# Weights in other areas, a ring of four weight slots, and the second product one block behind the first

## The reference

```python
x = x + L0_xcond(...)   # three rounds of slot attention
x = x + L0_ffn(...)     # 8 experts, top 2, all computed
x = x + L1_xcond(...)   # 16 heads of 64, over 512 + 77 keys
x = x + L1_ffn(...)     # 8 experts, each token to the one with the largest gate
x = x + L2_xcond(...)   # attention over itself, over the context, and a gated FFN
x = x + L2_ffn(...)     # 16 experts and a shared one
x = x + L3_xcond(...)   # 6 layers: attention, cross attention, FFN
x = x + L3_ffn(...)     # half of the tokens through an FFN
```

```python
logits = xf @ Wg + bg                      # xf: tokens, D = 128; Wg: 128 x 8
one_hot = jax.nn.one_hot(jnp.argmax(logits, axis=-1), e)
h = jax.nn.gelu(jnp.einsum('td,edh->eth', xf, W1), approximate=True)   # H = 512
y = jnp.einsum('eth,ehd->etd', h, W2)
out = jnp.einsum('etd,te->td', y, one_hot)
```

## Time and profile before

| what | value |
|---|---|
| median of 3 runs | 4170.21 us (4165.55 to 4171.18) |
| the profiled execution, its own time | 4145.95 us |
| its span from first to last instruction | 4144.1 us |
| mean granted TensorE clock | 0.949 |
| TensorE busy | 3599.2 us (87%) |
| VectorE busy | 2465.0 us (59%) |
| ScalarE busy | 2296.2 us (55%) |
| GpSimd busy | 1355.3 us (33%) |
| bytes moved by DMA | 146.41 MB, mean 35 GB/s |

### The profile page before, as it was taken

One profiled execution on the slowest core, in us unless ns is written; L12 is line 12 of the kernel. 1 busy time (PEld: TensorE's weight loads), 2 busy tenths in 40 slices (PEclk: granted clock), 3 DMA queues, 4 the chain that ended last, 5 costly groups with the idle time before them and its releaser, 6 DMA issues.

```text
span 4144.1 us, 56756 instructions
## 1 busy us (share of the span) xinstructions
PE 3599.2 (87%) x22327; PEld 1596.7 (39%) x22327; DVE 2465.0 (59%) x4758; ACT 2296.2 (55%) x3200; POOL 1355.3 (33%) x1355
## 2 busy tenths in 40 slices
PE   5699999899568988998895889898999998988886
PEld 4477433333443344334552233233333332333333
DVE  6732444544225345543658877777778677777754
ACT  4543554454124554545321766777767676776683
POOL 5500233333224511441003234344343442433411
PEclk8699999999799999999896999999999999999998
DMA  2000000000330010001111101111111110110100
GB/s 118 1 21 1 31 16 22 6 16 22 128 109 11 17 32 27 16 17 56 39 27 44 36 25 38 52 27 45 43 32 40 43 47 25 43 47 25 41 12 16
DMA packets 126956, 146.41 MB, mean 35 GB/s; under 512 B 36141, under 2 KB 107637, under 8 KB 124866
## 3 DMA queue, kind: packets, MB, share of 16 engines
q1 hardware_dynamic: 125664, 140.67, 11.5%
q0 software_dynamic: 1024, 2.10, 0.2%
HBM read 74.63 MB, written 6.43 MB: 20 GB/s over the span
## 4 chain that ended last, share of the span: by engine, by line
PE 59%; DVE 22%; ACT 8%; POOL 5%; DMA 3%; issue 3%; SPq 1%; POOLq 0%; DVEq 0%; ACTq 0%
PE ps L1903 6%; PE ps L1919 6%; PE ps L2114 6%; DVE c1sm L2862 4%; DVE c0sm L2862 4%; PE ps L2031 3%; PE ps L1823 3%; PE ps L1815 3%; PE ps L2100 3%; ACT wB L2358 2%; PE ps L2058 2%; PE ps L1951 2%; PE ps L1844 2%; PE ps L2158 2%; POOL c1m L3043 2%
## 5 line engine op out<-in xcount | busy, mean ns | idle before, releaser
L2358 ACT ACTIVATE wB<-ps 128x1024 f32<-128x1024 f32 (+1 forms) x762 | 762.1, 1022 | 270.0 <-PE ps L2100 263.8
L2862 DVE TENSOR_REDUCE c1sm<-ps 128x2 f32<-128x1024 f32 x384 | 456.6, 1220 | 128.1 <-PE ps L2058 125.3
L2862 DVE TENSOR_REDUCE c0sm<-ps 128x2 f32<-128x1024 f32 x384 | 453.2, 1219 | 97.2 <-PE ps L2058 95.3
L2656 DVE TENSOR_REDUCE c1sm<-ps 128x2 f32<-128x1024 f32 x128 | 151.7, 1220 | 194.0 <-PE ps L1868 192.8
L2656 DVE TENSOR_REDUCE c0sm<-ps 128x2 f32<-128x1024 f32 x128 | 152.5, 1221 | 172.3 <-PE ps L1868 171.3
L2358 ACT ACTIVATE c0m<-ps 128x1024 f32<-128x1024 f32 (+1 forms) x198 | 202.4, 1022 | 70.0 <-PE ps L2100 68.0
L2114 PE MATMUL ps<-wB,c1m 128*18 128x512 f32 (+1 forms) x1216 | 205.5, 611 | 1.1 <-DVE c1sm L2869 0.6
L1903 PE MATMUL ps<-c0ar 64*128 64x512 f32 (+1 forms) x640 | 178.1, 634 | 20.8 <-DVE c0sm L2656 9.1
L2100 PE MATMUL ps<-c0ar 64*128 64x512 bf16 (+1 forms) x864 | 167.0, 388 | 33.0 <-DVE c1sm L2862 14.4
L2100 PE MATMUL ps<-c1ar 64*128 64x512 bf16 (+1 forms) x864 | 165.3, 392 | 26.5 <-DVE c0sm L2862 9.2
L2992 POOL TENSOR_SCALAR c0sm<-c0sm 128x4 f32<-128x4 f32 x40 | 7.8, 194 | 547.9 <-DVE c0sm L2430 462.5
(11 more groups left out here) (918 smaller groups left out, 8268.1 us busy)
## 6 DMA issues: line engine op xcount, KB each, us to landing
c0ar<-c0m SPq DMA_DIRECT2D x216, 128.0 KB, 2.4
c1ar<-c0m SPq DMA_DIRECT2D x216, 128.0 KB, 2.4
c0m<-rscr SPq DMA_DIRECT2D x96, 128.0 KB, 2.9
c1m<-rscr SPq DMA_DIRECT2D x96, 128.0 KB
wA<-in_lay SPq DMA_DIRECT2D x6, 1346.0 KB, 5.6
c0ar<-in_x SPq DMA_DIRECT2D x15, 512.0 KB, 3.5
c1ar<-in_x SPq DMA_DIRECT2D x15, 512.0 KB
wA<-in_w SPq DMA_DIRECT2D x1, 4248.0 KB, 22.0
```

The source lines that it names most:

```text
L2358: e.activation(P.ap[0:n, :, :], u.ap[0:n, :].rearrange("p (a q) -> p a q", a=2), ACT.Exp, scale=S8).then_inc(*A(("P8", n0, s, k), free=[u]))
L2656: e.tensor_reduce(c.sm[:, 2 * (g % 2), 2 * j:2 * j + 2], u.ap.rearrange("p (h k) -> p h k", h=2)[:, :, 0:n], AX, ALU.max, negate=True).the ...
L2862: e.tensor_reduce(c.mneg[:, j, :, s // 4, s % 4], u.ap.rearrange("p (a k) -> p a k", a=2), AX, ALU.max, negate=True).then_inc(*V(free=[u]))
```

## The change

1. Stage 3 has a ring of four weight slots in place of three. The fourth takes the place of one of three token buffers and of free columns of the arena. The second product follows one block behind the first, not two.
2. `w4b` is split: the second attention's weights go to `wB`, the FFN's (`w4f`) to `wA` beside the first attention's (`w4a`). So `w4a` and `w4f` are loaded at the end of stage 1, `w4b` at the end of stage 2, `w5` goes to `wA`, the last FFN's `w7` to `wB`.
3. The layers of stage 6 use `wB` and `wA` in turn. Layer 0 is loaded at the end of stage 4 as before, layer 1 at the end of stage 5. The free columns that stage 6 shares out give seven buffers of 512 columns and not six.
4. A load of weights is now a step that the planner places by its clocks (`loads`), and a stream does not enter a stage before its load stands in the list.
5. The planner's numbers are new for all stages (`ORDER`; one of seven pairs of lines is shown).

Lines of the changed kernel from the planning part on have numbers up to 15 higher.

```diff
-    "3": dict(lag=0.0447, weight=0.2689, even=0, held=0.1381, table=0.6108, apart=9.6377, spread=0, seed=6349, bias=dict(TA=0.2, T=-0.615, S=1.124, VG=-1.263, TVb=-0.505, TAV=0.396, TV=1.124, V=0.115, A=0.392, G=-0.208), turns=((155, 662, 1.0), (397, 673, 0), )),
+    "3": dict(lag=0.0447, weight=0.2689, even=0.0203, held=0.1381, table=0.6108, apart=9.6377, spread=0, seed=6349, bias=dict(TA=0.2, T=-0.615, S=1.124, VG=-1.263, TVb=-0.505, TAV=0.396, TV=1.124, V=0.115, A=0.392, G=-0.208), turns=((47, 359, 0.3), (155, 662, 1.0), (397, 673, 0), )),
...
-        W4A, W4B, W5, W7 = view(wB, W4A_COLS), view(wA, W4B_COLS), view(wB, W5_COLS), view(wA, W7_COLS)
-        WL = [view(wA[:, k * LCOLS:(k + 1) * LCOLS], LAY_COLS) for k in range(2)]
+        W4A, W4B, W5, W7 = view(wA, W4A_COLS), view(wB, W4A_COLS), view(wA, W5_COLS), view(wB, W7_COLS)
+        W4F = view(wA[:, 4224:], W4F_COLS)
+        lay_at = [wB[:, 0:LCOLS], wA[:, 0:LCOLS]]
+        WL = [view(a, LAY_COLS) for a in lay_at]
         SEL = wA[:, 7200:8224]
...
-            r.B = Bufs([a[:, o:o + 512].rearrange("p (k d) -> p k d", k=4) for o in (1024, 1536, 2560)])
-            r.wring = [a[:, 5376 + 1024 * k:6400 + 1024 * k] for k in range(3)]
+            r.B = Bufs([a[:, o:o + 512].rearrange("p (k d) -> p k d", k=4) for o in (1024, 1536)])
+            r.wring = [a[:, o:o + 1024] for o in (2560, 5376, 6400, 7424)]
...
-        VC = [wA[0:NCTX, 2 * LCOLS + 1024 + 864 * k:2 * LCOLS + 1888 + 864 * k].rearrange("p (b q r) -> p b q r", b=NB, q=8)
+        VC = [wA[0:NCTX, LCOLS + 864 * k:LCOLS + 864 + 864 * k].rearrange("p (b q r) -> p b q r", b=NB, q=8)
...
-        spare = [[wA[:, 0:WA_COLS], 2 * LCOLS + 2752], [wB, 0], [areas[0][:, 0:5632], 0], [areas[1][:, 0:5632], 0],
+        spare = [[wA[:, 0:WA_COLS], LCOLS + 1728], [wB, LCOLS], [areas[0][:, 0:5632], 0], [areas[1][:, 0:5632], 0],
...
+        PACK = {"1": "w1", "2": "w2", "3": "w3", "4": "w4a", "5": "w5"}
+
+        def loads(pack, area, f):
+            yield from do("load", pack, area, f, chain=[("S", .4)], after=max(plan.clock[k] for k in "TAVG"))
+            issued.add(pack)
...
+                while PACK[name] not in issued:
+                    yield
                 if name not in begun:
                     begun[name] = c
                     if name != "1":
                         plan.stage(name)
-                    emit("gate", {"1": ("w_w1", "w1"), "2": ("w_w2", "w2"), "3": ("w_w3", "w3"), "4": ("w_w4a", "w4a"),
-                                  "5": ("w_w5", "w5")}[name])
+                    emit("gate", ("w_" + PACK[name], PACK[name]))
...
-                        emit("load", "w3", "wC", "1")
-                        emit("load", "w4b", "wA", "1")
+                        for pack, area in (("w3", "wC"), ("w4a", "wA"), ("w4f", "wF")):
+                            plan.spawn(loads(pack, area, "1"))
                     elif name == "2":
-                        emit("load", "w4a", "wB", "2")
+                        plan.spawn(loads("w4b", "wB", "2"))
                     elif name == "3":
                         emit("sel")
                     elif name == "4":
-                        for l in range(2):
-                            emit("lay0", l)
+                        emit("lay0", 0, "4")
                         plan.spawn(init6())
+                    elif name == "5":
+                        emit("lay0", 1, "5")
 
         def attn64(c, w, q, qkey, segs, yb, tz, AO):
...
-            for i in range(15 + 2):
+            for i in range(15 + 1):
...
-                if i >= 2:
-                    k = i - 2
+                if i >= 1:
+                    k = i - 1
...
-                emit("load", "w5", "wB", "4a")
-            if len(quarter) == 1:
+                plan.spawn(loads("w5", "wA", "4a"))
+            while "w4b" not in issued or "w4f" not in issued:
+                yield
+            if "4b" not in begun:
+                begun["4b"] = c
                 emit("gate", ("w_w4b", "w4b"))
+                emit("gate", ("w_w4f", "w4f"))
...
-                o = {"wA": wA, "wB": wB, "wC": wA[:, 7168:]}[area]
+                o = {"wA": wA, "wB": wB, "wC": wA[:, 7168:], "wF": wA[:, 4224:]}[area]
...
-            def lay0(l):
+            def lay0(l, f):
                 for s in (T, A, V, G):
-                    w.wait_ge(*s.at(("f", "4")))
-                e.dma_start(wA[:, l * LCOLS:(l + 1) * LCOLS], d["lay"][l]).then_inc(*D(f"w_l{l}")(("lay", l)))
+                    w.wait_ge(*s.at(("f", f)))
+                e.dma_start(lay_at[l], d["lay"][l]).then_inc(*D(f"w_l{l}")(("lay", l)))
 
             def lay(l, ms):
                 for m in ms:
                     w.wait_ge(*T.at(("fx2", m)))
                     w.wait_ge(*G.at(("yb", m)))
-                k = l % 2
-                e.dma_start(wA[:, k * LCOLS:(k + 1) * LCOLS], d["lay"][l]).then_inc(*D(f"w_l{l}")(("lay", l)))
+                e.dma_start(lay_at[l % 2], d["lay"][l]).then_inc(*D(f"w_l{l}")(("lay", l)))
 
             def lay7(ms):
                 for m in ms:
                     w.wait_ge(*T.at(("fx2", m)))
                     w.wait_ge(*G.at(("yb", m)))
-                e.dma_start(wA[:, 0:d["w7"].shape[1]], d["w7"]).then_inc(*D("w_w7")("w7"))
+                e.dma_start(wB[:, 0:d["w7"].shape[1]], d["w7"]).then_inc(*D("w_w7")("w7"))
 
             def i6m():
 
@@ -1956,10 +1970,10 @@
...
-W4B_COLS = [("wq", 1024), ("wk", 1024), ("wv", 1024), ("wo", 1024), ("bo", 128), ("w1", 1024), ("w2", 512),
-            ("b1", 8), ("b2", 128)]
+W4F_COLS = [("w1", 1024), ("w2", 512), ("b1", 8), ("b2", 128)]
```

33 lines of the change are left out of this document (17 added, 16 removed).

## The result

The changed kernel takes **4091.61 us** in the median (4091.37 to 4096.71, 4 runs). The kernel before, on the same chip, takes 4167.88 us (4153.54 to 4171.18, 4 runs). The ratio is 0.9826, 95% interval 0.9802 to 0.9851: 72 us or 1.7% less. The forecast was 4136 (4112 to 4164), so the direction was right and the gain was more than double the 34 us of the sum. The rivals "low clock stays", "the streams pay", "the gain is given back" and "it doesn't do what it says" are out; "more than counted" (4120) was the nearest, and it too was 28 us high.

The account below looks back on a forecast made before the run. TensorE's waits for expert weights in stage 3's three-slot ring were the limit. c1's stage 4 29 us earlier plus 5 us of c0's attention done ahead made 34 us, taken from the median 4170.21: 4136 us, range 4112 to 4164.

Parts of the forecast that it names:

- low clock stays: Rival 1, 8%: stage 3's single-stream gaps hold TensorE at 1.2 GHz, period 3.8 us, kernel 4160 us.
- the streams pay: Rival 2, 5%: stage 3's streams, one behind the other, no longer hide each other's loads; period 4.5 us, kernel 4184.
- the gain is given back: Rival 3, 12%: new orders of stages 2, 4, 5, 6 or streams further apart lose 26 or more of 34 us; 4165.
- it doesn't do what it says: Rival 5, chance included in rivals 1 and 2: stage 3's blocks 5 to 15 still wait for slots because SyncE is held.
- more than counted: Rival 4, 12%: stage 3's period of 2.0 us, an earlier start and a better stage 6 gain 50 us; 4120.
- P: Period of one stream's expert blocks in stage 3: larger of TensorE's work and L/2, taken as 2.5 us.
- L: Time in stage 3's weight ring from a freed slot to the product it feeds, 4.1 to 5.3 us.
- The stations of stage 3: Forecast times of c0's and c1's first and last products, ending with c1's stage 4 at 1235, 29 us earlier.
- The rest after c1's stage 4: From c1's stage 4 to the kernel's end: same distance as before, 2880 us, within 10.
- the term for the new orders of the stages: Planner's new numbers for stages 2, 4, 5 and 6: -10 to +10 us, taken as 0.
- The passage from the profile to the time: Whole kernel: 34 us saving gives a profiled span near 4110; taken from the median 4170.21 it gives 4136.
- The other edits counted at nothing: Moved weight loads (w4a, w4f, w4b, layer 1) counted at nothing; stage 6's extra buffer given -5 to 0 us.

Follow-up runs that it names:

- the second pair of profiles: Kernel before and changed kernel, each profiled again without an edit: spans 4156.1 and 4083.8 us.
- The earlier rank: Changed kernel with stage 3's bias TV at -1.0 instead of 1.124, c1's rank behind ten of c0's blocks: 4082.24 us, ratio 0.9795.

## Why the prediction was right or wrong

**What bounds stage 3: right.** The ring of weights was the limit. With it opened alone, in the kernel before, c0's first product to c1's stage 4 takes 145 us instead of 177, and the kernel is 43 us faster. TensorE's waits for weights were forecast under 15 us and are 5.8.

**The period: right, from a model that counts one block too many in the kernel before.** P = 2.5 us was forecast and 2.7 measured. The prediction put one block between freeing a slot and needing it in the kernel before; there is none, and with one the step there would have been about L, 4 to 5 us, and not the 8.4 that its own rows give. For the changed kernel the count of two is right. L in it is longer than the 4.1 to 5.3 us that were taken: from the end of the second product that frees the slot to the product that it feeds, blocks 5, 8, 12 and 15 of c0 took 6.4, 5.6, 4.9 and 5.5 us, of which half is 2.5 to 3.2. A second misreading has no effect: the idle times before c0's four blocks were 2.7, 3.6, 5.3 and 4.7 us, not all 4.7 to 5.3. The clock did come back over the blocks (products of 1.1 us), though 0.87 was granted in the window of c0's blocks and not the 0.95 that was named; rival 1 is out. The sums of rivals 1 and 2 leave out the 8 us for c0's attention that the forecast has: with them c1's end is 1128 + 26 P, and the streams would have paid from P = 3.6 and not 3.96.

**The stations of stage 3: right in kind.** By the sum against the trace: c0's first product 1079, measured 1072.3; from there to c0's last product 39 us, 40.2; from there to c1's first product 25.5, 22.2; c1's blocks 49.5, 42.9; from there to its stage 4 42, 40.4. Together that is c1's stage 4 at 1235 against 1218, 17 us. The two terms that were mis-sized most are the start, where the new numbers, put down at zero, have c0's rank 9 us earlier, and c1's blocks, for which I charged 12 us over the bare period (cold start and c0's attention) and 5 were paid.

**The rest after c1's stage 4: met in one pair of profiles, by luck.** Forecast 2880 within 10, measured 2876.9. But the kernel before itself has 2880.2 in one execution and 2888.3 in the next, and the second pair of profiles differs there by 20 us.

**The step that failed is the term for the new orders of the stages, put at 0 within -10 to +10.** The new numbers are worth 22 us in the kernel before (interval 13 to 31) and 13 by the ratios, 19 by the medians, in the changed one. The reasoning "no row prices that, so zero" was fair for its middle and too narrow for its width. A part of it could have been read from the order, in which both products of c0's gate (line 1741) now stand ahead of c1's output projection and not around it. I took c0's rank at its old time and never followed the new order back through stage 2. The rest is spread thinly and stays open. Beside it the ring was sized at 34 us and measured 43 by the ratio, 46 by the medians. In the profiles of the run with the ring alone and of the kernel before, its part at c1's stage 4 is 28 us, as forecast (29); after it come 9 us more, where the sum had 5 for work done ahead.

**The passage from the profile to the time failed too.** It is another way to cut the same 44 us, not to be added to the first. By its own terms the sum forecast a profiled span near 4110, and 4094.9 was measured: 15 us, the 17 of stage 3 less the 5 for work done ahead, plus the 3 of the rest. The other 29 us lie between profile and time. I wrote that the profiled execution of before was 24 us under its median, and took the saving from the median as if the 24 us were the same for both kernels. They are not. The changed kernel's profiled execution (4096.7) is 3 us above the mean of its eight, at their mean clock; that of the kernel before (4146) was 18 under the mean of 77, with a granted clock of 0.949 where 0.944 is the mean, and the median of three that I started from was 6.5 us above that mean. Two such executions at nearly one clock, 4146 at 0.949 and 4097 at 0.950, differ by 49 us; the means, at 0.944 and 0.951, by 70. By the slope of 2.5 us for 0.001 of clock, 17 of the 70 us are clock. That is an estimate from executions in which time and clock go together; it is not shown which drives which, nor which of the closed gaps brings the clock. The stage itself has more clock now, as the windows from 1000 to 1264 show, before and after:

```profile
1000.00:1264.00 264.00, 171.08 (x1033) 115.37 (x1030) 80.72 (x205) 65.15 (x100) 74.00 (x62) 0.83 0.31 97
```

```profile
1000.00:1264.00 264.00, 198.68 (x1244) 120.25 (x1241) 106.52 (x233) 91.95 (x136) 91.30 (x69) 0.88 0.30 100
```

0.05 more over 264 us would make 0.003 in the mean over 4100 us. In this pair it is lost again from 1400 to 2180, where the same two profiles have 0.96 and 0.93, so their means are nearly equal.

**The other edits counted at nothing: not contradicted.** Layout, planned loads, split `w4b`, layer weights in other places and the seventh buffer: 2 us by the medians and 11 by the ratios, not to be told from nothing. Layer 1's weights are issued at 2125.8, and TensorE doesn't wait for them at their first use at 2145.6.

**The order of the streams.** The prediction was right that the new order puts one stream after the other and opens a gap (25 us forecast, 20.1 of waiting measured). It did not foresee that either half of the ring edit alone would bring 38 to 42 of the 43 to 46 us.

**Sum of causes:** ring 43 to 46 us, planner's numbers 13 to 22, layout 2 to 11 (not told from nothing), against the 67 to 72 that were measured. The earlier rank gains about 14 more, with 12 us less of waiting between the streams and c0's rank 3.6 us earlier; it is not shown how the 14 divide between the two.

## What to carry to other kernels

In a ring, count the blocks between the instruction that frees a slot and the one that needs it: none left makes the step the whole latency plus the work (8.4 us here), one makes it the latency (4.0), two half of it (2.7). Once one such block is there, look at what else the loads' queue and the order of the streams do: here the second such block left the time where it was within the noise, while a wait of 26.5 us came up between the streams. And before a saving worked out in a profile is taken from a median, compare the profile's granted clock with that of ordinary executions of the same kernel: here the profile of before had 0.005 more clock than their mean and was 18 us under it, half of the 34 us that were forecast.

## What the runs showed of the hardware

- The mean granted clock of one and the same program varies from 0.939 to 0.951 between executions, and its time with it from 4170.4 to 4144.6 us at these two ends. A stretch in which TensorE is 90% busy can have all of its clock in one execution and 0.83 in the next.
- A load of 512 KB lands in 3.5 us at the median for c0 in the kernel before, in 4.1 us with the fourth slot alone, in 4.4 with the shorter distance alone and in 4.8 with both, where c0 takes 512 KB every 2.7 us and took them every 8.4 us alone: the latency rises by a third, and the rate threefold.
- The Trainium skill, TensorE: Matmul & The Clock Gate, HAM oscillation, says that in its thin-M kernel the wait for a DMA before each tile puts the array back at half clock each time. The runs agree where the wait is long (5.64 us, then a product of 2.07 us). With shorter waits they show both: waits of 0.8 to 2.8 us before every block left products of 1.2 us in most steps of the slots-only run, but in the kernel before a wait of 2.66 us was followed by a product of 2.08 us.
